# Four engines around a selective scan: Norm's sum in a tile of its own, z first in a unit, u ahead of the output, and the softplus correction on GpSimd

## The chip, the cores and the metric

The kernel runs on 1 core of one Trainium2 chip. The metric is the device time of one execution in microseconds; the time before is 16161.65, the median of 3 runs (16158.87 to 16184.59).

## The reference

A patch embedding with text tokens appended gives 16 sequences of L = 324 tokens and width 192. Then comes a stack of 16 Mamba layers, and behind it a mixture of experts. The change lies in the layers alone:

```python
h = rmsnorm(x, nw)
u, z = split(einsum('blh,ch->blc', h, in_w))         # 384 channels each
u = silu(causal_conv(u, cw, cb))                     # 4 taps
proj = einsum('bli,ci->blc', u, xp_w)                # dt_r (48), B (16), C (16)
dt = softplus(einsum('blr,ir->bli', dt_r, dtw) + dtb)
# for each t:  h = exp(dt * A) * h + dt * u * B;  y = sum over n of h * C
y = (y + u * D) * silu(z)
x = x + einsum('bli,hi->blh', y, ow)
```

The state has 384 channels x 16 n. All is float32.

## The kernel before

**Units and steps.** `run_layers` works through 256 units, one sequence in one layer each (`u`, L * IT = 972 elements wide). Inside a unit run 16 steps (`n`). The 384 x 16 states are laid on 128 partitions, 3 x 324 elements wide, in 16 tiles, so a step is one scan of 128 x 972. The hidden state of step n lies in `h[n % 8]`.

**A step on each engine.** ScalarE writes the decay exp(dt * A) into one of two PSUM tiles (L602, three instructions of 323 columns); decay n waits until scan n - 2 is done. GpSimd multiplies dt * u by B into `dbu` (L820, four tiles; dbu n waits for scan n - 4). VectorE scans (L770, behind decay n and dbu n) and then multiplies the state of step n - 1 by C (L779), C being broadcast over partitions by TensorE into one PSUM tile for four steps at a time (L439, `te_bcast`). For the steps in `ON_POOL` GpSimd makes that product instead (L828), with a C from a DMA. TensorE adds up products in pairs (L452, `te_sum`). Behind scan 2 VectorE gates the previous unit's sum with silu(z) (L787).

**The projections.** Three units are in work at once: while unit u is scanned, the kernel makes z and the end of softplus for p = u + 1, u's projection, convolution, x projection and dt projection for k = u + 2, and Norm for j = u + 3. All of them pass through one PSUM bank, `pj`, in halves: TensorE fills it, ScalarE copies it out, and the next fill waits for that copy. So their order is a chain: TensorE's order is written out in `tensor_step`, ScalarE's in `scalar_step`, VectorE's in `vector_step`, GpSimd's in `gpsimd_step` and that of SP's copies in `sync_step`. Each engine works strictly in the order written, and counts semaphores (`reached`) to wait for the others.

**Softplus** of p is Relu(x) + log(1 + exp(-|x|)) with a correction for the rounding of 1 + e: ScalarE evicts |x| and Relu(x) (L697, L698), makes e (L704), its logarithm `dtu` (L708, between two table loads, beside Norm's logarithm) and 1 + e (`u_pre`, L712). VectorE makes (u_pre - 1) - dtu (L794, `ve_log_error`), and GpSimd adds and subtracts (L841, L845) and multiplies by u (L849). dt and dt * u go to HBM and come back repeated over partitions (`dt_rep`, `dtu_rep`, four parts each), for the unit after.

## Time and profile before

| | us |
|---|---|
| median of 3 runs | 16161.65 |
| lowest, highest | 16158.87, 16184.59 |
| the profiled execution's own time | 16150.05 |
| its span, first to last instruction | 16148.2 |
| busy VectorE / TensorE / GpSimd / ScalarE | 85% / 84% / 83% / 70% |
| mean granted clock of TensorE | 0.903 of 2.4 GHz |

Durations below come from that one profiled execution. In its rows DVE is VectorE, PE is TensorE (PEld its weight loads), ACT ScalarE, POOL GpSimd and SP SyncE, whose queue issues the copies. L602 is line 602 of the kernel before. The duration of an instruction includes its fill and drain, so two in a row start closer together than the duration says. A mark like [1.46 <-ACT ps L602] says that the engine sat idle for 1.46 us and what ended it.

### The profile page before, as it was taken

How to read it: one execution, taken by the hardware profiler on the slowest of the kernel's cores; microseconds unless marked ns; L12 is line 12 of the kernel's file. 1: busy time of each engine (PE TensorE's matmuls, PEld its weight loads, DVE VectorE, ACT ScalarE, POOL GpSimd, SP SyncE). 2: the span in 40 equal slices, each digit the busy share in tenths (PEclk: the TensorE clock that was granted, in tenths of full speed). 3: DMA queues.
4: the chain of work that ended last, by engine and by line, in shares of the span. 5: the costliest groups of instructions: out<-in, count | busy, mean ns of one | idle time of the engine just before them, and what ended most of it. 6: DMA issues, size and time to landing. Idle time of an engine off the chain costs nothing. (4 is left out here: it accounts for less than half of the span.)

```text
span 16148.2 us, 205785 instructions
## 1 busy us (share of the span) xinstructions
PE 13519.5 (84%) x52202; PEld 6684.0 (41%) x52202; DVE 13797.9 (85%) x9806; ACT 11298.1 (70%) x21632; POOL 13365.1 (83%) x6095
## 2 busy tenths in 40 slices
PE   6888888888888888888888888888888888887689
PEld 4334434433343343343434334444434433434367
DVE  2999999999999999999999999999999999993643
ACT  3777777777777777777777777777777777773111
POOL 1999999999999999999999999999999999990023
PEclk7989999999999999989999998888989999997799
DMA  2333333333333333333333333333333333331022
GB/s 71 114 118 110 112 122 108 115 112 120 108 116 119 112 111 118 114 110 124 108 115 111 121 109 113 118 114 111 109 123 108 115 115 117 110 119 32 9 52 58
DMA packets 714479, 1703.22 MB, mean 105 GB/s; under 512 B 89033, under 2 KB 369462, under 8 KB 714162
## 3 DMA queue, kind: packets, MB, share of 16 engines
q1 hardware_dynamic: 693666, 1685.54, 31.4%
q0 software_dynamic: 19968, 15.98, 0.6%
q14 instruction: 109, 0.89, 0.0%
q10 hardware_dynamic: 720, 0.55, 0.0%
q8 instruction: 16, 0.26, 0.0%
HBM read 1414.96 MB, written 286.74 MB: 105 GB/s over the span
## 5 line engine op out<-in xcount | busy, mean ns | idle before, releaser
L820 POOL TENSOR_TENSOR dbu<-dtu_rep,b_rep 128x972 f32<-128x972 f32 x4096 | 9131.1, 2250 | 1066.6 <-DVE h L770 1041.0
L770 DVE TENSOR_TENSOR_SCAN h<-ps,dbu 128x972 f32<-128x972 f32 x4096 | 8825.4, 2169 | 1050.6 <-ACT ps L602 1049.6
L602 ACT ACTIVATE ps<-dt_rep,A_cur 128x323 f32<-128x323 f32 x12288 | 5881.6, 521 | 987.0 <-DVE h L770 806.6
L452 PE MATMUL ps<-h,fold 128*32 128x486 f32 x16400 | 4149.9, 668 | 78.2 <-DVE h L779 77.1
L779 DVE TENSOR_TENSOR h<-h,ps 128x972 f32<-128x972 f32 x3329 | 3800.2, 1142 | 105.2 <-PE ps L439 102.4
L828 POOL TENSOR_TENSOR h<-h,c_rep 128x972 f32<-128x972 f32 x769 | 1964.0, 2554 | 2.2 <-DVE h L770 2.2
L452 PEld LDWEIGHTS ps<-h,fold 128*32 128x32 f32 x16400 | 854.7, 119 | 2453.0 <-issue 2002.0
L530 PE MATMUL ps<-u_raw,w_cv 128*128 128x162 f32 (+7 forms) x8256 | 1801.9, 371 | 2.8 <-ACT u_raw L638 1.5
L530 PEld LDWEIGHTS ps<-u_raw,w_cv 128*128 128x128 f32 x8256 | 1359.4, 190 | 458.4 <-ACT u_pre L645 115.7
L1632 POOL DMA_INDIRECT e_rows<-n_rows,e_ix x96 | 96.9, 1010 | 1306.0 <-issue 1213.8
L439 PE MATMUL ps<-c_rows,sel_c 16*128 16x324 f32 x2048 | 882.6, 512 | 332.6 <-DVE h L779 332.5
L516 PE MATMUL ps<-x_norm,w_u 96*128 96x324 f32 (+1 forms) x4128 | 987.4, 383 | 202.1 <-ACT u_raw L638 196.2
L481 PE MATMUL ps<-x_norm,w_z 96*128 96x324 f32 (+1 forms) x4112 | 1011.6, 390 | 168.9 <-ACT z_pre L626 168.2
L550 PE MATMUL ps<-u_act,w_x 128*128 128x324 f32 x1548 | 538.1, 488 | 575.1 <-ACT u_act L653 568.1
L498 PE MATMUL ps<-y_gated,w_o 128*96 128x324 f32 x3084 | 1008.4, 466 | 0.0
L481 PEld LDWEIGHTS ps<-x_norm,w_z 96*128 96x128 f32 x4112 | 677.6, 195 | 624.9 <-issue 273.5
L516 PEld LDWEIGHTS ps<-x_norm,w_u 96*128 96x128 f32 x4128 | 664.6, 190 | 517.6 <-ACT u_raw L638 259.8
L632 ACT COPY x_T<-ps 96x324 f32 (+1 forms) x514 | 218.2, 424 | 922.8 <-PE ps L498 922.8
L559 PE MATMUL ps<-xp_rows,w_dt 49*128 49x162 f32 (+1 forms) x2064 | 696.0, 467 | 169.3 <-ACT xp_rows L689 165.4
L645 ACT COPY u_pre<-ps 128x486 f32<-128x486 f32 x516 | 290.9, 564 | 673.9 <-PE ps L530 673.8
L439 PEld LDWEIGHTS ps<-c_rows,sel_c 16*128 16x128 f32 x2048 | 315.7, 192 | 1004.1 <-DVE h L779 834.1
L496 PE MATMUL ps<-x_T,ident 96*96 x1028 | 405.9, 476 | 388.0 <-ACT z_pre L626 386.2
(171 smaller groups left out, 14794.0 us busy)
## 6 DMA issues: line engine op xcount, KB each, us to landing
dtu_rep<-dtu_rows SPq DMA_DIRECT2D x1028, 486.0 KB, 4.0
dt_rep<-dt_rows SPq DMA_DIRECT2D x1028, 486.0 KB, 6.6
b_rep<-b_rows SPq DMA_DIRECT2D x1028, 162.0 KB, 2.6
dt_rows<-dt SPq DMA_DIRECT2D x257, 486.0 KB, 2.7
dtu_rows<-dtu SPq DMA_DIRECT2D x257, 486.0 KB, 2.7
c_rep<-b_rows SPq DMA_DIRECT2D x770, 162.0 KB, 6.0
w_cv<-in_w_cv SPq DMA_DIRECT2D x17, 768.0 KB, 8.0
b_rows<-xp_rows SPq DMA_DIRECT2D x258, 40.5 KB, 6.0
```

The costliest lines, as they stand in the source:

```text
L439: pe.matmul(c_ps, sel_c[64:80, q, :], c_rows[par][64:80, :], start=True, stop=True).then_inc(s_cbc, 1)
L452: mm = pe.matmul(y_ps[32 * r:32 * r + 32, half, :], fold[:, :], src[:, half * YW:(half + 1) * YW], start=(m in (0, 1)), stop=(m < 0))
L481: mm = pe.matmul(pj[:, lo:hi], w_z[:, c, it * 128:it * 128 + 128], x_norm[par][:, c, t:t + hi - lo], start=(c == 0), stop=(c == 1))
L498: mm = pe.matmul(pj[0:HC, 0:L], w_o[:, it, half * HC:(half + 1) * HC], y_gated[:, it, :], start=False, stop=(it == IT - 1))
L516: mm = pe.matmul(pj[:, lo:hi], w_u[:, c, it * 128:it * 128 + 128], x_norm[par][:, c, t:t + hi - lo], start=(c == 0), stop=(c == 1))
L530: mm = pe.matmul(pj[:, lo + skip:hi], w_cv[:, it * KC + KC - 1 - back, :], u_raw[:, it * L + t + skip - back:it * L + t + hi - lo - back], ...
L559: mm = pe.matmul(pj[:, lo:hi], w_dt[:, it * 128:it * 128 + 128], xp_rows[0:RB, t:t + hi - lo], start=True, stop=True)
L602: ins = act.activation(decay[s % 2][:, it * L + 1:(it + 1) * L], dt_rep[:, s % NR, it, 1:L], ACT.Exp, scale=A_cur[:, it * N + s:it * N + s ...
L770: dve.tensor_tensor_scan(h[s % RING][:, :, :].rearrange("p i t -> p (i t)"), decay[s % 2], dbu[s % DRING][:, :, :].rearrange("p i t -> p ( ...
L779: dve.tensor_tensor(h[s % RING][:, :, :], h[s % RING][:, :, :], c_ps.unsqueeze(1).broadcast_to([128, IT, L]), ALU.mult).then_inc(s_prod, 1)
L820: pool.tensor_tensor(dbu[s % DRING][:, :, :], dtu_rep[:, r, :, :], b_rep[:, q, :].unsqueeze(1).broadcast_to([128, IT, L]), ALU.mult).then_ ...
L828: pool.tensor_tensor(h[s % RING][:, :, :], h[s % RING][:, :, :], c_rep[:, at, :].unsqueeze(1).broadcast_to([128, IT, L]), ALU.mult).then_i ...
```

## The change

`ON_POOL` goes from three steps to two, so VectorE makes 14 products of a unit instead of 13. The log error leaves VectorE: ScalarE makes (1 + e) - 1 with a second Identity (`u_pre` again, bias -1), and GpSimd has four operations on dt instead of three, behind dbu 3, 5, 6 and 7. Norm's sum gets a tile `ss` and a ScalarE copy of its own (`se_ss`), and both the matmul and the copy move to steps 10 and 11 of the unit before; the logarithm reads `ss`. TensorE takes z at steps 0 and 1, u at 2 and 3, the output at 4 and 5, the convolution at 6 and 7, skip at 8, Norm's sum at 10, x projection at 11 and dt at 12 and 13 (before: Norm's sum 0, z 1 and 2, output 3 and 4, u 5 and 6, skip 7, convolution 8 and 9, x projection 12, dt 13 and 14). ScalarE's copies follow that order. SP loads dt_rep 0 and 1 among the dtu_rep parts rather than behind them. The diff, cut to what works in the loop (left out: one memset of -1, the new semaphore, raised counts, first uses ahead of the loop):

```diff
-ON_POOL = (3, 7, 13)
+ON_POOL = (5, 12)
...
         sq = sb("sq", [HC, 2, L])
+        ss = sb("ss", [HC, L])
         rstd = sb("rstd", [HC, L])
...
         def te_sum(pe, u, m):
...
             reached(pe, s_prod, by_vector(u, 2 * m + 1))
-            if (2 * m + 1) % N in ON_POOL:
+            if not {2 * m % N, (2 * m + 1) % N}.isdisjoint(ON_POOL):
                 reached(pe, s_pprod, by_pool(u, 2 * m + 1))
...
         def te_z(pe, p, par, half):
...
                 wait(pe, s_wz, 16 * (layer(p) + 1))
-                reached(pe, s_lnss, p + 3)
+                reached(pe, s_dtev, 2 * p + 2)
             else:
...
-        def te_out(pe, u, half, lone=False):
+        def te_out(pe, u, half, a1=True):
...
                 wait(pe, s_wo, 16 * ((u + B - 1) // B + 1))
-                if lone:
+                if a1:
+                    reached(pe, s_ur, 2 * u + 6)
+                else:
                     reached(pe, s_dtev, 2 * u + 4)
-                else:
-                    reached(pe, s_zev, 2 * u + 4)
             else:
...
-        def te_u(pe, k, par, half, scan, b1):
+        def te_u(pe, k, par, half, b1):
             if half == 0:
...
                 wait(pe, s_wu, 16 * (layer(k) + 1))
-                if scan:
-                    reached(pe, s_oev, 2 * k - 2)
-                elif b1:
+                if b1:
                     reached(pe, s_zev, 2 * k)
                 else:
-                    reached(pe, s_lnss, k + 2)
+                    reached(pe, s_ssev, k + 2)
             else:
...
-        def te_conv(pe, k, half):
+        def te_conv(pe, k, half, scan):
...
             if half == 0:
+                if scan:
+                    reached(pe, s_oev, 2 * k - 2)
                 wait(pe, s_wc, 16 * (layer(k) + 1))
...
-        def te_ss(pe, j, b1):
-            reached(pe, s_sq, j + 1)
-            if b1:
-                reached(pe, s_dtev, 2 * j - 2)
+        def te_ss(pe, i, a1=True):
+            reached(pe, s_sq, i + 1)
+            if a1:
+                reached(pe, s_cvev, 2 * i - 2)
             else:
-                reached(pe, s_lnss, j)
+                reached(pe, s_ssev, i)
             for c in range(2):
...
         def te_xp(pe, k, par):
-            reached(pe, s_cvev, 2 * k + 2)
+            reached(pe, s_ssev, k + 3)
             reached(pe, s_ua, k + 1)
...
-        SUM_AT = {3: 0, 6: 1, 7: 2, 10: 3, 11: 4, 13: 5}
+        SUM_AT = {3: (0,), 5: (1,), 9: (2, 3), 11: (4,), 13: (5,)}
...
         def tensor_step(pe, u, par, scan=True, a1=True, b1=True):
...
                     te_bcast(pe, u, par, n // 4)
-                if n == 0:
-                    te_ss(pe, j, b1)
-                if n in (0, 1) and scan:
-                    te_sum(pe, u, n - 2)
-                if n in (1, 2) and b1:
-                    te_z(pe, p, 1 - par, n - 1)
-                if n in (3, 4) and scan:
-                    te_out(pe, u, n - 3)
-                if n in (5, 6) and a1:
-                    te_u(pe, k, par, n - 5, scan, b1)
-                if n in (8, 9) and a1:
-                    te_conv(pe, k, n - 8)
-                if n == 12 and a1:
+                if n == 1 and scan:
+                    te_sum(pe, u, -2)
+                    te_sum(pe, u, -1)
+                if n in (0, 1) and b1:
+                    te_z(pe, p, 1 - par, n)
+                if n in (2, 3) and a1:
+                    te_u(pe, k, par, n - 2, b1)
+                if n in (4, 5) and scan:
+                    te_out(pe, u, n - 4)
+                if n in (6, 7) and a1:
+                    te_conv(pe, k, n - 6, scan)
+                if n == 10:
+                    te_ss(pe, j + 1, a1)
+                if n == 11 and a1:
                     te_xp(pe, k, par)
-                if n in (13, 14) and a1:
-                    te_dt(pe, k, n - 13)
-                if scan and n in SUM_AT:
-                    te_sum(pe, u, SUM_AT[n])
-                if n == 7 and scan:
+                if n in (12, 13) and a1:
+                    te_dt(pe, k, n - 12)
+                for m in SUM_AT.get(n, ()) if scan else ():
+                    te_sum(pe, u, m)
+                if n == 8 and scan:
                     te_skip(pe, u, par, 0)
...
                 reached(act, s_ua, k)
-                reached(act, s_d1, k)
+                reached(act, s_dt, 4 * k - 2)
             act.copy(half_of(u_pre, half), pj).then_inc(s_cvev, 1)
...
         def se_silu(act, k, par, b1):
...
+        def se_ss(act, i):
+            reached(act, s_ss, i + 1)
+            reached(act, s_lnss, i)
+            act.copy(ss[:, :], pj[0:HC, 0:L]).then_inc(s_ssev, 1)
...
         def se_log_ss(act, j):
-            reached(act, s_ss, j + 1)
+            reached(act, s_ssev, j + 1)
             reached(act, s_xn, j)
-            act.activation(rstd[:, :], pj[0:HC, 0:L], ACT.Ln, bias=cst["eps"][0:HC, 0:1], scale=1.0 / H).then_inc(s_lnss, 1)
+            act.activation(rstd[:, :], ss[:, :], ACT.Ln, bias=cst["eps"][0:HC, 0:1], scale=1.0 / H).then_inc(s_lnss, 1)
...
         def se_dt(act, k, half):
...
             if half == 0:
-                reached(act, s_sp, 3 * k)
+                reached(act, s_sp, 4 * k)
                 wait(act, s_dst[0], 16 * k)
...
             elif step == 1:
-                reached(act, s_sp, 3 * p + 1)
+                reached(act, s_sp, 4 * p + 1)
                 wait(act, s_dst[1], 16 * p)
...
             else:
-                reached(act, s_d1, p)
+                reached(act, s_dt, 4 * p - 2)
                 reached(act, s_ua, p + 1)
                 act.activation(u_pre[:, :], exp_x[:, :], ACT.Identity, bias=cst["one"][:, 0:1]).then_inc(s_sp, 1)
+                reached(act, s_sp, 4 * p + 3)
+                act.activation(u_pre[:, :], u_pre[:, :], ACT.Identity, bias=cst["minus_one"][:, 0:1]).then_inc(s_sp, 1)
...
         def se_c_rows(act, p, par):
...
                     se_softplus(act, p, 0)
+                    se_z(act, p, 0)
                 if n == 1:
...
                     act.preload_act_table_set(MAIN_SET)
-                if n in (2, 3) and b1:
-                    se_z(act, p, n - 2)
                 if n == 2:
+                    if b1:
+                        se_z(act, p, 1)
                     se_rstd(act, j)
                     se_copy_nw(act, j)
-                if n == 2 and b1:
-                    se_softplus(act, p, 2)
-                if n in (4, 5) and scan:
-                    se_out(act, u, n - 4)
+                    if b1:
+                        se_softplus(act, p, 2)
+                if n in (3, 4) and a1:
+                    se_ur(act, k, n - 3)
                 if n == 4 and b1:
                     se_c_rows(act, p, other)
+                if n in (5, 6) and scan:
+                    se_out(act, u, n - 5)
                 if n == 5 and a1:
                     se_copy_cb(act, k)
-                if n in (6, 7) and a1:
-                    se_ur(act, k, n - 6)
                 if n == 6:
                     se_weighted_x(act, j, other)
-                if n == 8:
+                if n == 7:
                     se_sq(act, j + 1)
-                if n in (10, 11) and a1:
-                    se_conv(act, k, n - 10)
+                if n in (8, 9) and a1:
+                    se_conv(act, k, n - 8)
+                if n == 10 and a1:
+                    se_silu(act, k, par, b1)
+                if n == 11:
+                    se_ss(act, j + 1)
                 if n == 12 and a1:
-                    se_silu(act, k, par, b1)
-                if n == 13 and a1:
                     se_xp(act, k)
-                if n in (14, 15) and a1:
-                    se_dt(act, k, n - 14)
+                if n in (13, 14) and a1:
+                    se_dt(act, k, n - 13)
...
         def ve_product(dve, u, s):
...
-            if s % 4 == 0:
+            if s == min(i for i in range(s // 4 * 4, N) if i not in ON_POOL):
                 reached(dve, s_cbc, 4 * u + s // 4 + 1)
...
-        def ve_log_error(dve, p):
...
-            reached(dve, s_sp, 3 * p + 3)
-            dve.scalar_tensor_tensor(out=dtu[:, :], in0=u_pre[:, :], scalar=-1.0, in1=dtu[:, :],
-                                     op0=ALU.add, op1=ALU.subtract).then_inc(s_d1, 1)
...
         def vector_step(dve, u, par, scan=True, a1=True, b1=True):
...
                         ve_product(dve, u, n - 1)
-                if n == 3 and b1:
-                    ve_log_error(dve, p)
...
         def ge_dt(pool, p, par, step):
...
             if step == 0:
-                reached(pool, s_sp, 3 * p + 1)
+                reached(pool, s_sp, 4 * p + 1)
                 pool.tensor_tensor(dt[:, :], dt[:, :], exp_x[:, :], ALU.add).then_inc(s_dt, 1)
             elif step == 1:
-                reached(pool, s_dt, 3 * p + 1)
-                reached(pool, s_d1, p + 1)
-                pool.tensor_tensor(dt[:, :], dt[:, :], dtu[:, :], ALU.subtract).then_inc(s_dt, 1)
+                reached(pool, s_dt, 4 * p + 1)
+                reached(pool, s_sp, 4 * p + 4)
+                pool.tensor_tensor(dt[:, :], dt[:, :], u_pre[:, :], ALU.subtract).then_inc(s_dt, 1)
+            elif step == 2:
+                reached(pool, s_dt, 4 * p + 2)
+                pool.tensor_tensor(dt[:, :], dt[:, :], dtu[:, :], ALU.add).then_inc(s_dt, 1)
             else:
-                reached(pool, s_dt, 3 * p + 2)
+                reached(pool, s_dt, 4 * p + 3)
                 reached(pool, s_ua, p + 1)
...
                         ge_product(pool, u if n >= 4 else u - 1, (n - 4) % N)
-                if n == 4 and b1:
-                    ge_dt(pool, p, 1 - par, 0)
-                if n == 8 and b1:
-                    ge_dt(pool, p, 1 - par, 1)
-                    ge_dt(pool, p, 1 - par, 2)
-                if n == 10:
+                if n in (3, 5, 6, 7) and b1:
+                    ge_dt(pool, p, 1 - par, (3, 5, 6, 7).index(n))
+                if n == 11:
                     ge_x_norm(pool, u + 3, 1 - par)
...
         def sp_store_dt(sp, p, which):
...
-            reached(sp, s_dt, 3 * p + 2 + which)
+            reached(sp, s_dt, 4 * p + 3 + which)
             sp.sem_inc(s_go, 1)
...
             if b1:
-                for r in range(NR):
-                    sp_load_dtu(sp, u, r)
+                sp_load_dtu(sp, u, 0)
+                sp_load_dt(sp, u, 0)
+                sp_load_dtu(sp, u, 1)
+                sp_load_dtu(sp, u, 2)
+                sp_load_dt(sp, u, 1)
+                sp_load_dtu(sp, u, 3)
                 sp_load_b(sp, u, par, 3)
-                for r in range(2):
-                    sp_load_dt(sp, u, r)
             if reload:
...
                 se_sq(act, 0)
+                se_ss(act, 0)
                 all_units(scalar_step, act)
```

## Rows read from the trace of the kernel before

**Rows 1.** The page: its span, and busy us (share of the span) xinstructions

```profile
span 16148.2 us, 205785 instructions
PE 13519.5 (84%) x52202; PEld 6684.0 (41%) x52202; DVE 13797.9 (85%) x9806; ACT 11298.1 (70%) x21632; POOL 13365.1 (83%) x6095
```

**Rows 2.** Timeline of DVE (start, duration, instruction): first and last gate in the loop

```profile
379.78 1.14 DVE L787 TENSOR_TENSOR y_gated<-ps,z_act 128x972 f32<-128x972 f32 x1
...
14491.02 1.14 DVE L787 TENSOR_TENSOR y_gated<-ps,z_act 128x972 f32<-128x972 f32 x1
```

**Rows 3.** Groups by line: xcount, busy us, mean ns, idle before, releaser

```profile
L820 POOL TENSOR_TENSOR dbu<-dtu_rep,b_rep 128x972 f32<-128x972 f32 x4096 | 9131.1, 2250 | 1066.6 <-DVE h L770 1041.0 <-DMA dtu_rep<-dtu_rows 3.5
L770 DVE TENSOR_TENSOR_SCAN h<-ps,dbu 128x972 f32<-128x972 f32 x4096 | 8825.4, 2169 | 1050.6 <-ACT ps L602 1049.6
L828 POOL TENSOR_TENSOR h<-h,c_rep 128x972 f32<-128x972 f32 x769 | 1964.0, 2554 | 2.2 <-DVE h L770 2.2
...
L794 DVE SCALAR_TENSOR_TENSOR dtu<-u_pre,dtu 128x972 f32<-128x972 f32 x257 | 612.6, 2383 | 53.4 <-ACT u_pre L712 53.4
...
L712 ACT ACTIVATE u_pre<-exp_x,one 128x972 f32<-128x972 f32 x257 | 283.8, 1104 | 0.0
```

**Rows 4.** Timeline of DVE, one unit: scans 0, 1, 2, 4 and 5, 13, next 0

```profile
6016.04 2.18 DVE L770 TENSOR_TENSOR_SCAN h<-ps,dbu 128x972 f32<-128x972 f32 x1 [0.77 <-ACT ps L602]
...
6019.19 2.17 DVE L770 TENSOR_TENSOR_SCAN h<-ps,dbu 128x972 f32<-128x972 f32 x1
...
6023.88 2.18 DVE L770 TENSOR_TENSOR_SCAN h<-ps,dbu 128x972 f32<-128x972 f32 x1 [1.46 <-ACT ps L602]
...
6033.58 4.24 DVE L770 TENSOR_TENSOR_SCAN h<-ps,dbu 128x972 f32<-128x972 f32 x2
...
6061.63 2.18 DVE L770 TENSOR_TENSOR_SCAN h<-ps,dbu 128x972 f32<-128x972 f32 x1 [1.24 <-ACT ps L602]
...
6070.90 2.18 DVE L770 TENSOR_TENSOR_SCAN h<-ps,dbu 128x972 f32<-128x972 f32 x1 [0.81 <-ACT ps L602]
```

**Rows 5.** Timeline of ACT, same unit: decays 1, 2, z copy, u_pre, SiLU, decay 13

```profile
6016.75 1.42 ACT L602 ACTIVATE ps<-dt_rep,A_cur 128x323 f32<-128x323 f32 x3
...
6022.32 1.44 ACT L602 ACTIVATE ps<-dt_rep,A_cur 128x323 f32<-128x323 f32 x3
6023.77 0.56 ACT L626 COPY z_pre<-ps 128x486 f32<-128x486 f32 x1
...
6024.69 1.10 ACT L712 ACTIVATE u_pre<-exp_x,one 128x972 f32<-128x972 f32 x1
...
6055.18 1.28 ACT L653 ACT_TABLE_LOAD   x1
...
6060.16 1.44 ACT L602 ACTIVATE ps<-dt_rep,A_cur 128x323 f32<-128x323 f32 x3
```

**Rows 6.** Timeline of PE, same unit: broadcast, sum, z, output, convolution

```profile
6019.33 0.81 PE L439 MATMUL ps<-c_rows,sel_c 16*128 16x324 f32 x2 [2.33 <-DVE h L779]
6020.07 1.83 PE L452 MATMUL ps<-h,fold 128*32 128x486 f32 x8
6021.82 1.91 PE L481 MATMUL ps<-x_norm,w_z 96*128 96x324 f32 x8
...
6028.42 1.80 PE L498 MATMUL ps<-y_gated,w_o 128*96 128x324 f32 x6
...
6045.59 3.42 PE L530 MATMUL ps<-u_raw,w_cv 128*128 128x324 f32 x16
```

**Rows 7.** Timeline of PE, another unit: the same broadcast and z

```profile
3083.67 1.44 PE L439 MATMUL ps<-c_rows,sel_c 16*128 16x324 f32 x2 [2.68 <-DVE h L779]
...
3088.43 2.86 PE L481 MATMUL ps<-x_norm,w_z 96*128 96x324 f32 x8
```

**Rows 8.** A stretch: us, busy by engine, PE's granted clock, DMA share, GB/s

```profile
6063.00:6067.00 4.00, 4.00 (x13) 1.24 (x12) 4.00 (x4) 2.75 (x6) 4.00 (x3) 0.57 0.98 260
```

**Rows 9.** The page's DMA issues: xcount, KB each, median us to landing

```profile
dt_rep<-dt_rows SPq DMA_DIRECT2D x1028, 486.0 KB, 6.6
```

More of the change, by code:

```diff
@@ L158, in _ @@
                 dve.memset(cst["one"][:, :], 1.0)
+                dve.memset(cst["minus_one"][:, :], -1.0)
                 dve.memset(cst["ones96"][:, :], 1.0)
@@ L372, in run_layers @@
         s_ss = sem("s_ss")
+        s_ssev = sem("s_ssev")
         s_lnss = sem("s_lnss")
@@ L386, in run_layers @@
         s_sp = sem("s_sp")
-        s_d1 = sem("s_d1")
         s_dt = sem("s_dt")
@@ L1057, in _ @@
                               start=True, stop=False)
+                te_ss(pe, 0, a1=False)
                 all_units(tensor_step, pe)
@@ L1060, in _ @@
                 te_sum(pe, UNITS, -1)
-                te_out(pe, UNITS, 0, lone=True)
-                te_out(pe, UNITS, 1, lone=True)
+                te_out(pe, UNITS, 0, a1=False)
+                te_out(pe, UNITS, 1, a1=False)
             @block.scalar
@@ L1066, in _ @@
                 raise_counts(act, s_xw, s_exp, s_pA, s_pB, s_pN, s_ur, s_cvev, s_ua, s_za, s_xpev, s_dtev, s_sp,
-                             s_cq, s_oev, s_sq, s_lnss, s_rstd, s_zev)
+                             s_cq, s_oev, s_sq, s_ssev, s_lnss, s_rstd, s_zev)
                 act.preload_act_table_set(MAIN_SET)
@@ L1076, in _ @@
             def _(dve):
-                raise_counts(dve, s_scan, s_prod, s_gate, s_d1)
+                raise_counts(dve, s_scan, s_prod, s_gate)
                 for d in decay:
@@ L1764, in program @@
             "sel_c": sb("sel_c", [80, NQ, 128]), "fold": sb("fold", [128, 32]), "eps": sb("eps", [128, 1]),
-            "one": sb("one", [128, 1]),
+            "one": sb("one", [128, 1]), "minus_one": sb("minus_one", [128, 1]),
         }
```

## The prediction

> **What bounds the kernel now.** I began with the page: the span and the busy shares [rows 1]. VectorE (85%), TensorE (84%) and GpSimd (83%) lie within two points of each other and ScalarE is at 70%, so no engine is simply full, and the question is who waits for whom. The gates of the first and the last unit in the loop [rows 2] give the rhythm: (14491.02 - 379.78) / 255 = 55.34 us a unit. 256 units make 14167 us, and 16148.2 - 14167 = 1981 us lie outside the loop, which the change doesn't touch. Each 1 us of a unit is 256 us.
>
> The groups by line [rows 3] show where VectorE idles: 1050.6 us before the scans, nearly all behind ScalarE's decay, which is 4.1 us a unit. In the timeline of one unit [rows 4] a scan and the product behind it take 3.15 us (start to start), and a scan with no VectorE product behind it 2.07 (4.24 for two against 2.17 for one). So VectorE's own work is 13 x 3.15 + 3 x 2.07 + 1.06 (gate) + 2.3 (log error) = 50.5 us, and 55.34 - 50.5 = 4.8 us are stalls. The reader is to see in [rows 4] which scans stall: scan 2 by 1.46 and scan 13 by 1.24, both marked "ACT ps L602". Scan 0 comes 0.8 late in the same way (6070.90 against 6061.63 + 3.15 + 2.07 + 3.15).
>
> Why scan 2 stalls is in ScalarE's timeline [rows 5]: from decay 1 (6016.75) to decay 2 (6022.32) stand the decay, a table load, two logarithms and a table load, 5.57 us, where a scan step offers 3.15 and decay runs at most two scans ahead. Scan 13 has the same between decay 12 and 13 (SiLUs). GpSimd waits for the scans, not they for it [rows 3]: it's not the bound.
>
> **The change part by part.** I count time from the start of scan 0 of a unit, with each step at the fastest rows.
>
> *VectorE.* The log error goes: -2.3 us. One product comes back from GpSimd: +1.08. Its own work becomes 14 x 3.15 + 2 x 2.07 + 1.06 = 49.3 us, 1.2 less.
>
> *GpSimd.* One product less (2.55 mean), one dt operation more (2.25, by dbu, which has its shape) [rows 3]: 16 x 2.25 + 2 x 2.55 + 4 x 2.25 and about 1.6 for Norm's product (two thirds of the columns) = 51.7. It can be a bound only if a unit falls that low. Its second dt step now waits for ScalarE's second u_pre (12.5, below), with the dbu of step 6 queued behind: ready about 17 where scan 6 comes at 23. Hidden by 6 us.
>
> *ScalarE.* One copy of Norm's sum (under 0.5, by the larger z copy of [rows 5]) and one Identity (1.10, by L712). The copy stands behind decay 11, where ScalarE waits for TensorE anyway: nothing. The Identity stands between decay 2 and decay 3 and counts in full below. What the edit buys is that the dt pair comes one step sooner, so that ScalarE ends the unit early: from scan 11 on TensorE has xp (0.5 to 2.4; 6 matmuls, as the output's in [rows 6]), sum 4 (to 4.2), dt 0 (half a sum's matmuls, to 5.2), broadcast 3 behind product 11 (6.4 to 7.1), dt 1 (to 8.0), sum 5, z 0 (to 11.6). ScalarE has dt 0 from 5.3 to 6.2 (two operations), decay 14, dt 1 from 8.1 to 9.1, decay 15 to 10.5, decay 0 (it waits for scan 14, 10.6) to 12.4, exp and first z copy to 13.8, while scan 0 comes at 14.7. Decay 1 then starts at -0.9, and decay 2 ends at -0.9 + 1.43 + 4.13 + 1.44 = 6.1, against 6.3 for scan 2. **The stalls before scans 0 and 2 go**, 0.8 + 1.5 us in [rows 4].
>
> *TensorE's order* decides what comes instead. It works strictly in order. At step 1 it has: broadcast 0, both old sums, and only then the second half of z. Broadcast 0 waits for product 15, which ends when scan 1 starts (3.15). By [rows 6] the broadcast starts 0.14 later and takes 0.74, a sum 1.75, the second sum 1.75, z 1.91. The second z is there at 3.15 + 0.14 + 0.74 + 3.50 + 1.91 = **9.44**. ScalarE has finished decay 2 at 6.1 and stands at this copy for 3.4 us, with rstd, nw, both Identities and decay 3 queued behind. From [rows 5] z copy to u_pre is 0.92; two Identities 2.1; decay 1.44: decay 3 is ready at 13.95. Scan 3 could start at 6.3 + 4.2 = 10.5. **New stall: 3.45 us.** Before, the z copies stood behind decays 2 and 3 and the second half held nothing up.
>
> *From scan 3 (count anew)*: u 0 copied 0 to 0.5, u 1 0.6 to 2.5, sum 0 to 4.2, first output 4.2 to 6.6 (0.62 + 1.75, [rows 6]), broadcast 1 waits for product 3 (6.3) and ends 7.3, second output 7.3 to 9.7. ScalarE copies it 9.75 to 10.1, weighted x 0.92, decay 7 ends 12.5; scan 7 could start at 2 x 3.15 + 3.15 + 2.07 = 11.5. **Stall 0.95.** The broadcast and the output stand in each other's way here; before, step 3 was GpSimd's and it waited for product 2 alone. TensorE goes on: sum 1 to 11.4, first convolution 3.36 to 14.8, copy, second 15.45 to 18.95. ScalarE copies it (19.0), decay 10 to 20.9, table load + SiLUs + table load 5.0 [rows 5], decay 11 to 27.3. Scan 11 could start at 12.5 + 4 x 3.15 = 25.1. **Stall 2.25**, in the place of the 1.3 before scan 13. From scan 11 the unit ends 4 x 3.15 + 2.07 = 14.7 later.
>
> Sum at full clock: 49.3 + 3.45 + 0.95 + 2.25 = **56.0 us**, against 54.87 for an undisturbed unit before (scan 0 to scan 0 in [rows 4]: 6070.90 - 6016.04 = 54.86) and 55.34 in the mean.
>
> *The clock of TensorE.* The difference 55.34 - 54.87 = 0.5 is what half-rate stretches cost now. The granted clock fell to 0.57 in the mean of 4 us of this unit [rows 8], most of them at 1.2 GHz. What it costs at worst is in [rows 7]: behind 2.68 us of idleness (beside the row) broadcast, sum and z took 7.6 us (3083.67 to 3091.29) against 4.4 in [rows 6], 3.2 more: 2.3 in broadcast and sum, 0.95 in z. After the change the first z ends at -3.1 and TensorE idles until 3.3, **6.3 us in one piece**, over twice the gap of [rows 7], straight ahead of the very burst that ScalarE waits for, and the burst holds a second sum. Bounds: 0 (it doesn't fall in time), 3.2 + 1.6 = 4.8 (whole burst at 1.2 GHz). I take 2.2, between half of the 4 us of [rows 8] that lie at about half rate (1.7) and the row at 3.2, since the fall comes while it idles and has partly passed. The gap of 2.6 us before u 1 and the one before xp can do the same; I keep the 0.5 of before for these (bounds 0 and 2). The Trainium skill (TensorE: Matmul & The Clock Gate, HAM oscillation) states that a gap of idleness drops the clock so that each following burst starts cold; by that rule the whole burst is slow in nearly every unit, which gives 61.3 us and 17690. The idleness beside [rows 7] agrees in kind; that it holds for every such gap no row shows.
>
> *Queue order of the copies.* SP now issues dt_rep 0 as soon as decay 12 and dbu 12 are done, 12.8 us ahead of scan 0, with decay 0 at 3.8 ahead: 9 us, where landing takes 6.6 [rows 9]. Hidden, 2.4 to spare; if it were late, it would eat first into the 2.4 us by which decay 0 is early. The dtu loads behind it feed GpSimd, which has slack. One c_rep load less a unit: the DMA engines are a third busy, nothing. A weight reload is moved past nothing. The first te_ss and se_ss ahead of the loop and a memset: under 3 us once.
>
> **Sum.** 56.0 + 2.2 + 0.5 = 58.7 us a unit. 256 x 58.7 + 1981 = 17008 us of span. The profiled execution took 16150.05 with a span of 16148.2 (+2), and the median of the runs shown, 16161.65, is 12 above it: 17020 us.
>
> **The rivals.**
>
> (A, forecast, 0.58) second z waits and the clock makes it worse: 57.4 to 61 a unit, 16680 to 17600.
>
> (B, 0.22) second z waits but the clock hardly counts (0 to 0.9, as the mean cost of 0.5 before): 56.0 to 56.9, 16320 to 16560. For it: dense work follows the burst. Against: the gap is over twice that of [rows 7], which already cost 3.2.
>
> (C, other side, 0.09) the middle of the unit is shorter than I walk it. Scan 7's stall rests on TensorE handing over the second output 1.2 us after ScalarE asks, and half of scan 11's on the second convolution coming at 18.95 rather than at 17.8, when scan 8 is done. If TensorE is ahead there by 2 us (outputs and sums overlapping more than their starts in [rows 6] say) and its clock holds in the burst, 0.95 goes and 2.25 becomes about 1.0: 49.3 + 3.45 + 1.0 + 0.5 = 54.3 us, 15900. It decides where the three stalls together fall below 5.5 (55.34 - 49.3 - 0.5). For it: VectorE and GpSimd both have less to do. Against: the starts of [rows 6] leave TensorE no 2 us.
>
> (D, 0.09) the whole burst runs at 1.2 GHz in every unit (56.0 + 4.8 + 0.5 = 61.3), or the bursts of xp and dt do too: xp, sum 4 and dt 0 in a row (4.7 us) take 2.3 to 4.2 more by the ratios of [rows 7] to [rows 6], dt 0 is copied by 9 or later after scan 11, and decay 14 ends at 10.5 or later where scan 14 could start at 8.4: 61 to 63, 17600 to 18100. The skill's rule above, taken to its end, gives this case.
>
> (E, 0.02) within 0.2%, 55.2 to 55.5: needs the gains and losses to cancel. 0.2% is about what a measurement of this kernel can tell from no change.
>
> Range 16330 to 17550: it takes A but its top, most of B, and leaves C, D and E out (0.2). Faster 0.09, same 0.02, slower 0.89.
>
> **What the profile would show.** Right: scans 0 and 2 start without idle time, scan 3 is preceded by 3.5 us or more, scan 11 by about 2 and scan 7 by about 1, all behind L602's decay; ScalarE's largest wait is the second z copy, for TensorE, 3 us or more in each unit; TensorE idles about 6 us before broadcast 0, and its sums behind it take over 1.8 us in most units; VectorE's product count rises from 3329 by 256, L794 is gone. Wrong: scans 7 and 11 with under 1 us of idle time together (C); sums at 1.75 behind the gap (B); a stall before scan 14 (D). The prediction falls first if decay 2 isn't followed by a wait, and next by the size taken for the clock.

## The result and the profile after

The changed kernel takes 17712.02 us (17704.08 to 17723.51) against 16168.92 of the kernel before beside it: a ratio of 1.0954, 95% interval 1.0935 to 1.0973. The forecast was 17020 us with a range of 16330 to 17550, so the time lies 162 us above its top. The direction and the first cause were right; the size was not.

The page of the changed kernel, its span and busy us; it answers [rows 1]:

```profile
span 17715.7 us, 206450 instructions
PE 13619.6 (77%) x52206; PEld 6922.6 (39%) x52206; DVE 13600.6 (77%) x9806; ACT 11628.8 (66%) x22149; POOL 13129.8 (74%) x6096
```

VectorE does 197 us less and GpSimd 235 us less, and yet the span is 1567.5 us longer: on VectorE, 1765 us more are idle time. The first and the last gate in the loop, as in [rows 2]:

```profile
381.93 1.15 DVE L800 TENSOR_TENSOR y_gated<-ps,z_act 128x972 f32<-128x972 f32 x1
...
16044.66 1.17 DVE L800 TENSOR_TENSOR y_gated<-ps,z_act 128x972 f32<-128x972 f32 x1
```

(16044.66 - 381.93) / 255 = 61.42 us a unit, where it was 55.34; outside the loop little changed (17715.7 - 256 x 61.42 = 1992 us, before 1981). Groups by line, those of [rows 3] and three that wait:

```profile
L783 DVE TENSOR_TENSOR_SCAN h<-ps,dbu 128x972 f32<-128x972 f32 x4096 | 8920.0, 2178 | 2390.5 <-ACT ps L605 2365.7 <-POOL dbu L825 24.8
...
L833 POOL TENSOR_TENSOR h<-h,c_rep 128x972 f32<-128x972 f32 x513 | 1154.0, 2250 | 1.0 <-DVE h L783 1.0
...
L850 POOL TENSOR_TENSOR dt<-dt,u_pre 128x972 f32<-128x972 f32 x257 | 573.5, 2232 | 1399.2 <-ACT u_pre L722 1399.2
...
L722 ACT ACTIVATE u_pre<-u_pre,minus_one 128x972 f32<-128x972 f32 x257 | 283.9, 1105 | 8.4
L629 ACT COPY z_pre<-ps 128x486 f32<-128x486 f32 x514 | 283.8, 552 | 1024.2 <-PE ps L483 1024.2
```

The scans wait 2366 us for decays (1050 before). The z copies wait 1024 us, 4.0 us in each unit: the wait that the prediction named. GpSimd stands 5.4 us a unit at its second dt step, and the scans wait only 24.8 us in the whole run for it.

VectorE's timeline of one unit, the scans that stall (scans 3, 5, 6 and 7; [rows 4] before), with product 4, which waits for broadcast 1:

```profile
9046.81 2.18 DVE L783 TENSOR_TENSOR_SCAN h<-ps,dbu 128x972 f32<-128x972 f32 x1 [4.06 <-ACT ps L605]
...
9053.46 2.18 DVE L783 TENSOR_TENSOR_SCAN h<-ps,dbu 128x972 f32<-128x972 f32 x1 [0.26 <-ACT ps L605]
9057.40 1.17 DVE L792 TENSOR_TENSOR h<-h,ps 128x972 f32<-128x972 f32 x1 [1.76 <-PE ps L441]
9058.77 2.18 DVE L783 TENSOR_TENSOR_SCAN h<-ps,dbu 128x972 f32<-128x972 f32 x1 [0.20 <-POOL dbu L825]
9062.78 2.18 DVE L783 TENSOR_TENSOR_SCAN h<-ps,dbu 128x972 f32<-128x972 f32 x1 [1.83 <-ACT ps L605]
```

ScalarE at the second z copy, and the chain behind it (compare [rows 5]):

```profile
9036.82 1.44 ACT L605 ACTIVATE ps<-dt_rep,A_cur 128x323 f32<-128x323 f32 x3
9042.29 0.56 ACT L629 COPY z_pre<-ps 128x486 f32<-128x486 f32 x1 [4.03 <-PE ps L483]
...
9043.21 1.10 ACT L720 ACTIVATE u_pre<-exp_x,one 128x972 f32<-128x972 f32 x1
9044.34 1.10 ACT L722 ACTIVATE u_pre<-u_pre,minus_one 128x972 f32<-128x972 f32 x1
9045.35 1.43 ACT L605 ACTIVATE ps<-dt_rep,A_cur 128x323 f32<-128x323 f32 x3
```

TensorE in the same unit: xp, then (half a unit later) the last work before the long gap, broadcast 0, both sums, second z, and u 0, u 1, sum 0 ([rows 6, 7] before):

```profile
9016.78 3.53 PE L552 MATMUL ps<-u_act,w_x 128*128 128x324 f32 x6 [3.45 <-ACT ss L674]
...
9027.14 1.91 PE L483 MATMUL ps<-x_norm,w_z 96*128 96x324 f32 x8
9035.36 1.44 PE L441 MATMUL ps<-c_rows,sel_c 16*128 16x324 f32 x2 [6.31 <-DVE h L792]
9036.73 3.48 PE L454 MATMUL ps<-h,fold 128*32 128x486 f32 x16
9040.14 2.11 PE L483 MATMUL ps<-x_norm,w_z 96*128 96x162 f32 x8
9042.91 1.91 PE L516 MATMUL ps<-x_norm,w_u 96*128 96x324 f32 x8 [0.65 <-ACT z_pre L629]
9047.33 3.55 PE L516 MATMUL ps<-x_norm,w_u 96*128 96x162 f32 x8 [2.51 <-ACT u_raw L641]
9050.81 3.46 PE L454 MATMUL ps<-h,fold 128*32 128x486 f32 x8
```

The gap ahead of the burst is 6.31 us, as walked (6.3). Behind each of the three gaps (3.45, 6.31, 2.51) the work runs at 1.2 GHz, and so in every unit of this execution away from the loop's two ends, where each unit takes 61.43 to 61.45 us. The stretches over these three, with TensorE's granted clock behind the five engines' busy times, as in [rows 8]:

```profile
9016.80:9020.20 3.40, 3.40 (x6) 1.82 (x6) 3.40 (x3) 1.19 (x3) 1.61 (x1) 0.51 0.24 33
...
9035.30:9041.00 5.70, 5.64 (x23) 1.99 (x23) 5.70 (x5) 2.93 (x5) 4.79 (x3) 0.54 0.07 25
9047.30:9054.00 6.70, 6.67 (x16) 2.76 (x16) 6.44 (x5) 3.77 (x8) 6.70 (x4) 0.51 0.00 0
```

### The profile page after: what moved, and what is told of

Its sections match the earlier page's. It is cut to its first block and busy times, and to the rows that moved or that the text cites. A ratio compares the mean times of both kernels' runs of the same rounds, so it can differ in the third digit from the quotient of the medians.

```text
span 17715.7 us, 206450 instructions
## 1 busy us (share of the span) xinstructions
PE 13619.6 (77%) x52206; PEld 6922.6 (39%) x52206; DVE 13600.6 (77%) x9806; ACT 11628.8 (66%) x22149; POOL 13129.8 (74%) x6096
## 5 line engine op out<-in xcount | busy, mean ns | idle before, releaser
L792 DVE TENSOR_TENSOR h<-h,ps 128x972 f32<-128x972 f32 x3585 | 4109.7, 1146 | 581.4 <-PE ps L441 581.4
L454 PE MATMUL ps<-h,fold 128*32 128x486 f32 x16400 | 3656.3, 742 | 4.2 <-DVE h L792 4.2
L516 PE MATMUL ps<-x_norm,w_u 96*128 96x324 f32 (+1 forms) x4128 | 1412.5, 504 | 812.9 <-ACT u_raw L641 644.0
L850 POOL TENSOR_TENSOR dt<-dt,u_pre 128x972 f32<-128x972 f32 x257 | 573.5, 2232 | 1399.2 <-ACT u_pre L722 1399.2
L552 PE MATMUL ps<-u_act,w_x 128*128 128x324 f32 x1548 | 909.6, 760 | 890.9 <-ACT ss L674 890.9
L454 PEld LDWEIGHTS ps<-h,fold 128*32 128x32 f32 x16400 | 715.8, 128 | 2218.5 <-issue 1783.2
L516 PEld LDWEIGHTS ps<-x_norm,w_u 96*128 96x128 f32 x4128 | 913.7, 257 | 1201.2 <-ACT u_raw L641 707.7
L833 POOL TENSOR_TENSOR h<-h,c_rep 128x972 f32<-128x972 f32 x513 | 1154.0, 2250 | 1.0 <-DVE h L783 1.0
L552 PEld LDWEIGHTS ps<-u_act,w_x 128*128 128x128 f32 x1548 | 476.4, 328 | 1239.2 <-issue 1230.9
L629 ACT COPY z_pre<-ps 128x486 f32<-128x486 f32 x514 | 283.8, 552 | 1024.2 <-PE ps L483 1024.2
```

Source lines behind the costliest of these rows:

```text
L454: mm = pe.matmul(y_ps[32 * r:32 * r + 32, half, :], fold[:, :], src[:, half * YW:(half + 1) * YW], start=(m in (0, 1)), stop=(m < 0))
L516: mm = pe.matmul(pj[:, lo:hi], w_u[:, c, it * 128:it * 128 + 128], x_norm[par][:, c, t:t + hi - lo], start=(c == 0), stop=(c == 1))
L552: mm = pe.matmul(pj[0:XROWS, 0:L], w_x[:, it, :], u_act[par][:, it, :], start=(it == 0), stop=(it == IT - 1))
L792: dve.tensor_tensor(h[s % RING][:, :, :], h[s % RING][:, :, :], c_ps.unsqueeze(1).broadcast_to([128, IT, L]), ALU.mult).then_inc(s_prod, 1)
L833: pool.tensor_tensor(h[s % RING][:, :, :], h[s % RING][:, :, :], c_rep[:, at, :].unsqueeze(1).broadcast_to([128, IT, L]), ALU.mult).then_i ...
```

## The experiments

Stalls are worked out from VectorE's timeline: the time from one scan's start to the next, less what it takes without a stall (3.15, or 2.07 where GpSimd makes the product, 4.21 before scan 3 with the gate). The table gives means over units 10 to 244 of a trace, in us; a wait of product 4 shows before scan 6, one of product 8 before scan 10, and the last column is scan 0 to scan 0. Unit lengths in the text are (span - 1981) / 256, which also holds what a run adds outside the loop, up to 0.2 us a unit.

| run | scan 2 | 3 | 5 | 6 | 7 | 10 | 11 | 14 | unit, shortest to longest |
|---|---|---|---|---|---|---|---|---|---|
| changed | 0.04 | 4.19 | 0.34 | 2.15 | 1.94 | 0.62 | 1.77 | 1.06 | 61.44, 61.43 to 61.45 |
| 1 | 0.17 | 1.91 | 0.40 | 1.90 | 1.94 | 0.62 | 1.77 | 1.70 | 59.73, 59.56 to 59.91 |
| 2 | 0.98 | 2.31 | 0 | 0 | 1.16 | 0.62 | 1.77 | 0.02 | 56.22, 55.43 to 57.11 |
| 3 | 0.24 | 0.12 | 0.05 | 0.25 | 1.30 | 0.62 | 1.77 | 0.93 | 54.61, 53.47 to 57.36 |
| 7 | 1.65 | 3.15 | 0 | 0.85 | 1.94 | 0.62 | 1.77 | 2.12 | 61.44, 61.43 to 61.45 |
| 13 | 0.04 | 4.15 | 0 | 0 | 1.16 | 0.62 | 1.77 | 0.97 | 58.03, 58.02 to 58.04 |
| 14 | 0.87 | 3.45 | 0.20 | 1.47 | 1.94 | 0.62 | 1.77 | 0.02 | 59.73, 59.08 to 60.40 |

**1 and 2. TensorE kept busy in its gaps.** A tile of zeros times the identity, added to the sum of y, which it leaves as it is:

```diff
+        def fill(pe, count, alone=False):
+            for _ in range(count):
+                pe.matmul(y_ps[:, 0, 0:128], zero[:, :], ident[:, :], start=alone, stop=alone)
...
+                if scan and n == 1:
+                    fill(pe, 24)
                 if scan and n % 4 == 1:
                     te_bcast(pe, u, par, n // 4)
```

> The changed kernel with 24 matmuls by a tile of zeros (128 columns each, about 5 us at 2.4 GHz) put where TensorE idles 6.3 us ahead of broadcast 0; they add zero and move nothing else. Theory: the half-rate burst behind that gap is a cost of its own. Then broadcast, sums and second z take 4.6 us from their start instead of 6.9, scan 3 stalls 1.8 us instead of 4.2, and a unit falls from 61.4 to about 59 if the other half-rate stretches stay (57 to 59.5): 16550 to 17200 us. Rival (the order alone costs, the clock is hidden): within 0.5 us a unit of the changed kernel, 17600 to 17800.

17323.82 us, a ratio of 1.0701 (1.0683 to 1.0719): 59.9 us a unit, 1.55 less than the changed kernel and above the 17200 that the theory allowed. TensorE's timeline has the same burst at full clock:

```profile
6044.85 5.52 PE L572 MATMUL ps<-ident,zero 128*128 128x128 f32 x48
6051.32 0.81 PE L442 MATMUL ps<-c_rows,sel_c 16*128 16x324 f32 x2 [0.95 <-DVE h L800]
6052.06 1.85 PE L455 MATMUL ps<-h,fold 128*32 128x486 f32 x16
6053.84 1.91 PE L484 MATMUL ps<-x_norm,w_z 96*128 96x162 f32 x8
```

From scan 1's start, which is where product 15 ends, to the end of z are 4.56 us (6051.19 to 6055.75) instead of 7.03 (9035.22 to 9042.25). Two kinds of unit take turns here. In the longer one the stall before scan 3 is 1.8, as expected, and the one before scan 14 went from 1.06 to 2.4; in the shorter one they are 2.1 and 1.0, with 0.3 before scan 2. The rival (the order alone) falls.

> As before it, with the same kind of matmuls in the gap before u 1 (10) and before xp (12) too. Theory: all three half-rate stretches go; left are the stalls at full clock, 1.8 before scan 3, about 1 before scan 7 and about 2 before scan 11: 49.3 + 4.9 = 54.2 to 55 us a unit, 15850 to 16070, which is faster than the kernel before. Rival (the order alone costs): 17600 to 17800. Second rival (the order costs what I walked, 56.0 a unit at full clock): 16320.

16428.69 us, 1.0146 (1.013 to 1.0163), 56.4 us a unit, 5.0 less. The stretches over u 1 and xp went, and with them the waits before scans 5, 6 and 14. But 56.4 is not the expected 54.2 to 55: a half-rate stretch now lay over dt 1, sum 5 and in part the first z, which made the 24 matmuls late and delayed broadcast 0. The burst itself ran at full clock, and still 2.3 us stood before scan 3. The number agrees with my old walk (56.0) by chance; its parts don't.

**3. Second z early.** One thing moved:

```diff
-                if n in (0, 1) and b1:
-                    te_z(pe, p, 1 - par, n)
+                if n == 0 and b1:
+                    te_z(pe, p, 1 - par, 0)
+                    te_z(pe, p, 1 - par, 1)
```

> The changed kernel with one thing moved: TensorE makes the second half of z right behind the first, ahead of broadcast 0 and the two sums. Theory: ScalarE no longer waits behind decay 2, the stall before scan 3 (4.2 us a unit) falls under 0.5 and the 6.3 us gap is cut in two: 52.5 us a unit at full clock to 57.2 with the other stretches as they are, 15420 to 16650. Rival (scan 3 waits for the two Identities and Norm's operations, not for z): the stall before scan 3 stays above 2 us and the time above 17100.

16013.60 us, 0.9893 (0.9877 to 0.991): 54.8 us a unit, **1.1% faster than the kernel before**, clear of the noise. ScalarE no longer waits behind decay 2:

```profile
6005.43 1.44 ACT L606 ACTIVATE ps<-dt_rep,A_cur 128x323 f32<-128x323 f32 x3
6006.81 0.55 ACT L630 COPY z_pre<-ps 128x486 f32<-128x486 f32 x1
```

The stall before scan 3 is 0.12. What is left is 0.6 at product 8, 1.8 before scan 11, 1.3 before scan 7, 0.9 before scan 14 and 0.2 before scan 2. Both sums behind broadcast 0 still run at half rate in every unit, behind gaps of 0.3 to 2.0 us, but the z copy no longer waits for them. Of the 6.8 us from scan 0 to scan 0, 4.1 are that stall; most of the rest is at scans 5 to 7, since u 1 ran at half rate in only one unit of eight. And the gap of 3.45 us before xp, unchanged, was followed by xp at half rate in only half of the units:

```profile
6094.14 1.90 PE L552 MATMUL ps<-u_act,w_x 128*128 128x324 f32 x6 [3.45 <-ACT ss L675]
...
6150.55 3.41 PE L552 MATMUL ps<-u_act,w_x 128*128 128x324 f32 x6 [3.45 <-ACT ss L675]
```

**4.** 

> Both: second z early, and zero matmuls in the three gaps (6 before broadcast 0, 10 before u 1, 12 before xp). Theory: 52.5 to 53.5 us a unit, 15420 to 15680. Rival (once z is early the clock no longer matters): within 0.5% of the kernel with z early alone.

16869.73 us, 1.0421 (1.0403 to 1.0438): a miss, 58.2 us a unit. The stall before scan 14 went, but again dt 1, sum 5 and the first z ran at 1.2 GHz, so the z copy held up decay 1 (1.9 us before scan 2), and the 10 matmuls before u 1 took 4.6 us instead of 2.4 and delayed it. So work put in one gap moves a half-rate stretch to another.

**5 and 6. xp ahead of Norm's sum**, both with z early; run 6 also moves sum 1 behind the second convolution and ScalarE's convolution copies one step up. The moves of xp:

```diff
-                if n == 10:
-                    te_ss(pe, j + 1, a1)
-                if n == 11 and a1:
+                if n == 10 and a1:
                     te_xp(pe, k, par)
+                if n == 11:
+                    te_ss(pe, j + 1, a1)
...
-                if n == 11:
-                    se_ss(act, j + 1)
-                if n == 12 and a1:
+                if n == 11 and a1:
                     se_xp(act, k)
+                if n == 12:
+                    se_ss(act, j + 1)
```

> The kernel with z early, and the x projection ahead of Norm's sum instead of behind it (TensorE at steps 10 and 11, ScalarE's copies at 11 and 12). Theory: xp no longer waits 3.4 us for Norm's copy behind the SiLUs, so TensorE has no gap there, the half-rate stretch over xp, sum 4 and dt goes, and with it the stall before scan 14 (0.9 us a unit): 53.5 to 54.4 us a unit, 15680 to 15910. Rival (that stall comes from the distance of xp to dt, not from its start): within 0.3% of z early alone, 15960 to 16060.

16839.07 us, 1.0418 (1.04 to 1.0435), a miss: 58.0 us. Scan 14's stall did go and xp ran at full clock. But this is the stretch over dt 1, sum 5 and the first z in that kernel:

```profile
6045.00:6051.30 6.30, 6.20 (x15) 1.91 (x15) 6.17 (x5) 3.78 (x9) 6.30 (x4) 0.55 0.91 344
```

It delays the z copy and so decay 1, for 1.6 us before scan 2, and a second one over u 1 brings back 2.0 before scan 6.

> As before it, and sum 1 behind the second convolution, ScalarE's copies of the convolution one step earlier (7 and 8). Theory: the stall before scan 11 (1.8 us, and 0.6 at product 8 ahead of it) hangs on the second convolution's copy, which holds decay 10 and the SiLUs; it comes 1.5 us sooner: 52 to 53.3 us a unit, 15300 to 15630. Rival (the SiLUs with their table loads between decays 10 and 11 are the stall, whenever they start): less than 0.3 us a unit, under 80 us, against the xp-first kernel.

16561.41 us, 1.0248 (1.0231 to 1.0265): 56.9 us. Scan 11's stall only went from 1.77 to 1.56, and broadcast 2 came later instead (1 us before scan 9). The 1.1 us gained on the kernel above lie mostly at scans 2 and 6, so neither case came; the theory on the convolution isn't borne out.

**7. The old queue order.** `sp_load_dtu` 0 to 3, b_rep 3 and `sp_load_dt` 0 and 1, as in the kernel before.

> The changed kernel with SP's old order (all four dtu_rep loads, b_rep 3, then dt_rep 0 and 1). Theory: decay 0 has over 2 us to spare, so nothing moves: within 0.2% of the changed kernel, 17670 to 17750. Rival (dt_rep 0 lands late for the earlier decay 0): 0.5 to 1.5 us a unit more, 17840 to 18100.

17718.34 us, 1.0961 (1.0943 to 1.098): no difference, and 61.48 us a unit. The stalls lie elsewhere, though (the table has them), because in this trace dt 1, sum 5 and the first z run at half rate as well:

```profile
6199.01 1.70 PE L561 MATMUL ps<-xp_rows,w_dt 49*128 49x162 f32 x4 [0.55 <-ACT dt L706]
6200.64 3.46 PE L454 MATMUL ps<-h,fold 128*32 128x486 f32 x8
6204.03 2.95 PE L483 MATMUL ps<-x_norm,w_z 96*128 96x324 f32 x8
```

That isn't shown to come from the queue order. The changed kernel's four executions have mean granted clocks of 0.858, 0.858, 0.811 and 0.81 at 17704 to 17724 us, and this kernel's have 0.809, 0.809, 0.859 and 0.858 at 17715 to 17723: each kernel shows both clocks, at the same time. The changed kernel was traced in an execution of the first kind and this one in one of the second, so the two traces can differ in this alone. It is likely, though with one trace of each not shown, that where the stretches lie differs between executions of one kernel while the unit takes 61.44 us all the same; the stalls listed for the changed kernel are those of the first kind.

**8. The old softplus correction.** The second Identity goes, `ve_log_error` comes back behind product 2, GpSimd has three operations.

> The changed kernel with the softplus correction as before: the log error on VectorE behind product 2, one Identity on ScalarE, three dt operations on GpSimd. Theory: the chain second z, Identities, decay 3 loses 1.1 us, and VectorE's 2.3 us lie where it waits for TensorE's broadcast 1 anyway: about 60.3 us a unit, 17430 (17350 to 17600). Rival (VectorE's work counts in full): 62.6 us a unit, 18000.

16844.13 us, 1.0419 (1.0402 to 1.0437), 58.05 us, far below both cases: **3.4 us a unit less for taking 1.1 from ScalarE and giving VectorE its log error back**. TensorE shows what went: the gap before u 1 is 1.37 instead of 2.51, and both u 1 and sum 0 run at full clock:

```profile
6012.91 1.91 PE L517 MATMUL ps<-x_norm,w_u 96*128 96x324 f32 x8 [0.65 <-ACT z_pre L630]
6016.19 1.91 PE L517 MATMUL ps<-x_norm,w_u 96*128 96x162 f32 x8 [1.37 <-ACT u_raw L642]
6018.03 1.82 PE L455 MATMUL ps<-h,fold 128*32 128x486 f32 x8
```

The log error itself is not what it was. In the kernel before it took 2.38 us in 256 of 257 cases, always with GpSimd working beside it; here GpSimd waits for it, and it takes 1.16 ([rows 3] has the mean before):

```profile
6018.83 1.17 DVE L806 SCALAR_TENSOR_TENSOR dtu<-u_pre,dtu 128x972 f32<-128x972 f32 x1
```

So what the change moved off VectorE costs it 1.1 us where GpSimd is idle, and 2.3 where GpSimd is busy.

**9.** `ON_POOL = (3, 7, 13)` in the changed kernel. 

> The changed kernel with GpSimd's products at steps 3, 7 and 13 as before. Theory: the chain of TensorE and ScalarE sets the unit and VectorE's product (1.08 us) is hidden in its waits: within 0.5 us a unit, 17590 to 17850. Rival (VectorE's work counts): 1.1 us a unit less, 17430. Second rival (broadcast 1 may start a product sooner and clears the stall before scan 7): 2 us less, 17200.

17546.63 us, 1.0858 (1.0839 to 1.0876): 60.8 us, 0.6 less, between the first two cases and below the first one's range. The gap before broadcast 0 was 2.7 to 5.4 us, and the units took 59.3 to 62.1 us.

**10 and 11. The second dt half ahead of broadcast 3**, with z early, and with xp first.

> The kernel with z early (54.8 us a unit), and the second dt half ahead of broadcast 3 on TensorE. Theory: the half-rate stretch over xp is untouched, the second dt half and what follows come up to 1 us sooner; a unit within 0.7 us of z early alone, 15850 to 16030. Rival (moving work there shifts a half-rate stretch onto the second z, as xp first did): 2 us or more a unit above, 16500 or more.

16840.01 us, 1.0421 (1.0404 to 1.0439): the rival's size, but not its place. The stretch fell on u 0, u 1 and sum 0 (3.61, 3.61 and 3.42 us each), behind gaps of 0.9 and 0.8 us, and the second z kept its full rate; 58.05 us a unit came out.

> The kernel with z early and xp first (58.0 us a unit, where the half-rate stretch lies on dt 1, sum 5 and z and delays decay 1), and the second dt half ahead of broadcast 3. Theory: what the earlier xp costs is where the half-rate stretch falls, through the gap of 1.8 us before broadcast 3; with that gap divided by the dt half the stall before scan 2 (1.6 us) shrinks and the unit falls to 54 to 56 us, 15800 to 16320. Rival (xp first costs by its order): 58.0 stays, 16830.

16403.24 to 16828.33 us over four runs; the runs of this kernel differ by 2.6% where others differ by 0.3% at most, and its units took 56.6 to 60.0 us. No reading rests on it.

**12. Output ahead of u.** 

> The changed kernel with the output at TensorE's steps 2 and 3 and u at 4 and 5, and ScalarE's copies so too. Theory: the order of the two costs nothing at full clock; the gap behind the first piece shrinks from 2.5 to 2.0 us, since an output half takes 0.5 longer than a u half. If 2.0 still drops the clock: 61.4 us a unit, 17650 to 17800. Rival (u ahead of the output is itself a cost, or 2.0 is short enough): 58 to 60 us, 16830 to 17350.

17055.73 us, 1.0554 (1.0537 to 1.0572), 58.9 us: the rival's size. The gap before the second output half is 1.82 us, and in half of the units that half still ran at 1.2 GHz (3.38 for 1.80), in the others it did not; u 1 and sum 0 stay near their full rate, and broadcast 1 came in time. The units took 57.4 to 60.8 us. Which of the two gave the 2.6 us, the order or the place of the stretch, this run doesn't separate.

**13 to 15.** The gap before u 1 alone, the gap before xp alone, and z early with the old softplus.

> The changed kernel with 10 zero matmuls in the gap between u 0 and u 1 alone, behind the gate. Theory: u 1 and sum 0 run at 2.4 GHz, broadcast 1 no longer keeps product 4 waiting 2.2 us and scans 5 and 7 lose 1.2 more: 57.8 to 58.5 us a unit, 16780 to 16960, the same as undoing the second Identity, which cures the same gap. Rival (the Identity costs by its place, the gap's clock little): above 60.5 us, 17470 or more.

16880.92 us, 1.0413 (1.0396 to 1.0431), 58.25 us (58.03 from scan 0 to scan 0): the theory. The waits before scans 5 and 6 went and scan 7's fell to 1.16, and the two Identities are still there:

```profile
6015.11 2.40 PE L572 MATMUL ps<-ident,zero 128*128 128x128 f32 x20
6017.78 1.91 PE L517 MATMUL ps<-x_norm,w_u 96*128 96x162 f32 x8 [0.28 <-ACT u_raw L650]
6019.62 1.83 PE L455 MATMUL ps<-h,fold 128*32 128x486 f32 x8
```

> The changed kernel with 12 zero matmuls in the gap before xp alone. Theory: the stall before scan 14 (1.1 us) goes: 60.4 us a unit, 17440 (17380 to 17520). Rival (as with xp first, the half-rate stretch moves onto dt 1, sum 5 and z, but z isn't early here and decay 0 has slack): within 0.3 us of the changed kernel, 17640 to 17780.

17310.52 us, 1.068 (1.0661 to 1.0698), 59.9 us: more than expected, 1.6 us a unit. Scan 14's stall (1.06) went. Two kinds of unit share the rest, one of 59.1 and one of 60.4 us; in the longer one dt 1, sum 5 and the first z run at half rate, and the decay 1 that they hold up costs 1.6 us before scan 2 of the next unit.

> Second z early and the softplus correction as before. Theory: with z early the gap before u 1 no longer halves the clock, so the Identity is worth no more than its 1.1 us, against VectorE's 2.3 us of log error: 54 to 56 us a unit, 15810 to 16320. Rival (the Identity costs 3 us wherever it is): 51.5 us, 15170.

16021.95 us, 0.989 (0.9871 to 0.9909), 54.8 us: the theory. With z early, the second Identity (1.1 us) is worth no more than VectorE's log error, which takes 1.16 us here too and not the 2.3 of the expectation. The gap before xp is 3.45 us and followed by half rate, but one of 2.3 us inside z is followed by z at full rate.

## Why the prediction was right in direction and short in size

- **VectorE 49.3 us of its own work, GpSimd no bound:** right. The 2.3 us for the log error were right for the kernel before, where GpSimd works beside it; run 8 has it at 1.16. Scans 0 and 2 start without a wait (0 and 0.04 in the changed kernel), so the stalls there are gone, as walked. In run 7's trace 1.65 us stand before scan 2.
- **The second z behind broadcast 0 and both sums:** right in mechanism, shown by run 3, which moves it alone and wins 6.7 us a unit. The term was mis-sized at both ends. At full clock I took two sums at 1.75 each; two sums one behind the other take 1.85 together (run 1, 6052.06), so z comes at 7.7 after scan 0 and not 9.4, and the stall is 1.8 (run 1, the longer units), not 3.45. Half rate adds 2.4 (4.2 in the changed kernel), near the 2.2 taken. Sum: 4.2 for a predicted 5.65.
- **Scan 7, 0.95:** 1.16 at full clock (run 13), 1.94 measured. **Scan 11, 2.25:** 1.77, with 0.62 at product 8 ahead of it, 2.4 together. Both walks hold.
- **The step that failed** is "I keep the 0.5 of before for these (bounds 0 and 2)": the gaps before u 1 and xp. The stalls behind them are 4.3 us a unit in the changed kernel, over twice the upper bound: 0.34 before scan 5, 2.15 at product 4, 0.8 of scan 7, 1.06 before scan 14. Filling the first gap alone takes away 3.4 us (61.44 to 58.03, run 13), filling the second alone 1.7 (61.44 to 59.73, run 14). I had the walk that shows the gap of 2.6 us and that TensorE has no slack from u 1 to the second convolution, and priced the stretch as a mean over the units of the old kernel, where in the new one every unit got it. The terms close: 49.3 + 4.2 + 1.2 (scan 7) + 2.4 (scan 11 with product 8) + 4.3 = 61.4.
- **The 0.5 was itself read wrongly.** It is the mean unit less one called undisturbed, the unit in which [rows 8] show a granted clock of 0.57. The units before run from 54.0 to 57.8 us, so if the stretches are what makes them differ, they cost at least 1.3 us a unit already there.
- **Case D** named the whole first burst or xp's and dt's, not u 1's. That 61.4 lies in its 61 to 63 is luck: of its parts, xp's came (1.06 in the stalls), and the u 1 stretch, which it doesn't have, is the larger one.
- **The Identity** at 1.1 us: its own duration was right (1105 ns), its price in the unit 3.4 (run 8). Run 13 keeps both Identities, fills the gap before u 1 and ends at the same 58.03, so the price lies in what follows that gap; in run 15, with z early, it is nothing.
- **The Trainium skill's rule** (TensorE: Matmul & The Clock Gate, HAM oscillation), taken to its end, gave 17690 in the prediction, and the measured time is 17712; but by other parts: it was worked out as 4.8 us on the first burst alone, where 2.4 fell there and 4.3 on the other two, and two sums took 1.7 us less than walked. So the number is near by luck. The trace agrees that half rate follows this kernel's three gaps in every unit; in run 3 xp ran at full rate behind the same gap of 3.45 us in half of the units.
- **Queue order:** nothing, right in the sum (run 7).

The parts at full clock, put together from runs 1, 13 and 14, are 49.3 + 1.8 + 1.16 + 0.62 + 1.77 = 54.6 us, and 55.2 with run 2's 2.3 before scan 3. That is an estimate: no run had all of a unit at full clock. It lies under the 55.34 of before, but that mean holds half-rate stretches too, and the shortest unit before took 54.0. So most of the loss is the clock's, and whether the order alone costs up to 1 us isn't shown. The prices of single gaps don't add, either: runs 1, 13 and 14 give 1.7, 3.4 and 1.7, run 2 with all three 5.2 (all from scan 0 to scan 0).

**Left open.** Why filling or moving a gap brought a half-rate stretch to dt 1, sum 5 and z in every unit of runs 2, 4 and 5, in half of those of run 14 and in none of run 13, wasn't settled, and run 7 has it without any gap filled. Why units end at the same few lengths (below) wasn't either; it means that a saving of 1 us can show as 3.4 or as nothing, so that no single run here prices a wait by itself. Nor was Norm's sum evicted by itself undone alone: its copy holds xp back for 3.45 us behind the SiLUs, and run 5, which took that away on top of z early, had its gain eaten by a stretch elsewhere.

## What to carry to other kernels

Walk the order of an in-order engine through one period, and mark each gap with what comes right behind it: a gap in front of work that someone waits for can cost twice, once by itself and once by the clock. Price such a stretch both ways, in no period and in every one, and let the range hold both; its mean in the old kernel says little about the new one. Then move the work that someone waits for out from behind the gap: run 3 kept the slow sums and won 6.7 us a unit, much of it because the z copy no longer waited for them. Don't price a small operation by one run: the same 1.1 us was worth 3.4 in run 8 and nothing in run 15.
